# Sixteen-wide heads: query projections without padding, and projections in narrower pieces

## What is computed

```python
def cross(x, ctx, Wq, bq, Wk, bk, Wv, bv, Wo, bo):      # layers 0 and 2
    xn = layernorm(x)                                    # (2, 1024, 256)
    Q, K, V = xn @ Wq + bq, ctx @ Wk + bk, ctx @ Wv + bv # heads of 16
    attn = softmax(Q_h @ K_h.T / 4)                      # 16 heads, 1024 x 77
    return concat(attn @ V_h) @ Wo + bo

def msa(x, w_qkv, w_proj):                               # layer 3
    q, k, v = split(x @ w_qkv)                           # heads of 16
    attn = softmax(q_h @ k_h.T * 0.25)                   # 16 heads, 1024 x 1024
    return concat(attn @ v_h) @ w_proj

x = x + tanh(g) * cross(layernorm(x), ctx, ...)          # layers 0 and 2
x = x + msa(layernorm(x), w_qkv, w_proj)                 # part of layer 3
```

## Time and profile before

| | |
|---|---|
| median of three runs | 3246.15 us (3243.53 to 3255.63) |
| the profiled execution's own time | 3252.0 us |
| its span | 3250.3 us |
| TensorE (PE) busy | 2932.5 us, 90% of the span |
| VectorE (DVE), ScalarE (ACT), GpSimd (POOL) busy | 1639.8, 1269.4, 1286.2 us |
| l0x, about | 5 to 157 us |
| l2x, about | 1500 to 1640 us |
| l3a, about | 2490 to 3015 us |

### The profile page before, as it was taken

How to read it: one execution, slowest core, us unless ns; L and a number is a source line. 1 busy time by engine, 2 the same in 40 slices (tenths; PEclk the granted TensorE clock), 3 DMA queues, 4 the chain that set the end, 5 groups by cost and what they waited for, 6 DMA issues and landing times. The chain is left out here.

```text
span 3250.3 us, 41502 instructions
## 1 busy us (share of the span) xinstructions
PE 2932.5 (90%) x15957; PEld 1574.7 (48%) x15957; DVE 1639.8 (50%) x3314; ACT 1269.4 (39%) x1769; POOL 1286.2 (40%) x1025
## 2 busy tenths in 40 slices
PE   7999899999999999697988999978887888988798
PEld 3565444444434444244466889843333222322587
DVE  4636555554555455485651112246552787786400
ACT  4443444334334443355521111124433465555232
POOL 2232366565666556701243222214656220010433
PEclk9999999999999999898998999989998899999999
DMA  1400000000000000000025455520001000000376
GB/s 55 115 27 28 11 6 6 11 6 6 10 6 6 6 6 1 27 1 29 1 83 192 180 204 199 214 79 5 1 14 33 11 14 7 7 14 1 131 239 174
DMA packets 76855, 175.72 MB, mean 54 GB/s; under 512 B 19549, under 2 KB 54290, under 8 KB 63860
## 3 DMA queue, kind: packets, MB, share of 16 engines
q0 software_dynamic: 21744, 118.63, 10.6%
q1 hardware_dynamic: 54916, 54.43, 5.5%
HBM read 141.70 MB, written 27.64 MB: 52 GB/s over the span
## 5 line engine op out<-in xcount | busy, mean ns | idle before, releaser
L1554 POOL TENSOR_TENSOR l1x_added<-l1x_added,l1x_probs 128x1024 f32<-128x1024 f32 x224 | 527.4, 2355 | 264.2 <-ACT l1x_probs L1825 198.5
L1922 DVE TENSOR_REDUCE l1x_tops<-l1x_ring 128x1 f32<-128x512 f32 x512 | 326.4, 685 | 195.3 <-PE l1x_ring L1634 194.8
L1153 DVE TENSOR_REDUCE l3a_halves<-l3a_ring 128x1 f32<-128x512 f32 x512 | 323.3, 683 | 88.1 <-PE l3a_ring L995 84.3
L1825 ACT ACTIVATE l1x_probs<-l1x_slots 128x1024 f32<-128x1024 f32 x256 | 262.0, 1024 | 239.4 <-PE l1x_slots L1678 237.6
L1112 ACT ACTIVATE l3a_probs<-l3a_slots 128x1024 f32<-128x1024 f32 x256 | 248.1, 1021 | 180.3 <-PE l3a_slots L1016 180.3
L1671 PE MATMUL l1x_slots<-l1x_Q,l1x_K 64*128 64x512 f32 x1152 | 311.0, 617 | 6.7 <-ACT l1x_probs L1823 5.5
L1693 PE MATMUL l1x_pv<-l1x_probs,l1x_V 128*64 128x512 f32 x1152 | 282.3, 606 | 0.0
L1016 PE MATMUL l3a_slots<-l3a_lifted,l3a_K 32*128 32x512 f32 x1024 | 151.6, 641 | 34.5 <-ACT l3a_probs L1112 33.6
L947 POOL TENSOR_TENSOR l3a_OT<-l3a_raw,l3a_rsum 128x512 f32<-128x512 f32 x16 | 20.3, 1268 | 403.5 <-DVE l3a_rsum L1184 403.5
L3561 DVE TENSOR_TENSOR l2f_hh<-l2f_sg,l2f_hid 128x256 f32<-128x256 f32 (+1 forms) x184 | 69.8, 380 | 213.0 <-ACT l2f_sg L3408 197.1
L3408 ACT ACTIVATE l2f_sg<-l2f_hid 128x256 f32<-128x256 f32 (+1 forms) x184 | 64.6, 352 | 286.0 <-PE l2f_hid L3324 276.2
(11 more groups left out here) (709 smaller groups left out, 5188.5 us busy)
## 6 DMA issues: line engine op xcount, KB each, us to landing
l1x_w<-in_l_qkv SPq DMA_DIRECT2D x16, 384.0 KB, 3.1
slots_in<-zeros SPq DMA_DIRECT2D x1, 4992.0 KB, 18.2
l2f_yg<-rows_out SPq DMA_DIRECT2D x8, 512.0 KB, 5.5
l2f_xg<-slots_in SPq DMA_DIRECT2D x15, 272.0 KB
slots_in<-zeros SPq DMA_DIRECT2D x1, 2944.0 KB, 17.9
x<-in_x SPq DMA_DIRECT2D x4, 512.0 KB, 8.7
l1f_w<-in_l_w SPq DMA_DIRECT2D x2, 1024.0 KB, 7.2
x<-x SPq DMA_DIRECT2D x4, 512.0 KB, 2.9
```

Of the source, the lines that this page charges most:

```text
L1153: nc.vector.tensor_reduce(halves[:, k % 2, col:col + 1], bank_of(banks[e]), AX.X, ALU.max).then_inc(s["bank_done"], 1)
L1554: ins = nc.gpsimd.tensor_tensor(added[h][:], added[h][:], probs[:, n % PROBS, :, :], ALU.add)
L1825: ins = nc.scalar.activation(p, s2[m % 2], ACT.Exp)
L1922: ins = nc.vector.tensor_reduce(tops[:, e * NT + t, h:h + 1], bank, AX.X, ALU.max)
```

## The change

Three parts.

1. Both cross attentions: from unit 4 on, the query projection uses dense weights `wq_dense` (new input `qd`), so one projection of 512 columns yields two units. Its result goes to `dense`, and SP spreads it with four DMAs per unit into Q, whose pads are those of the first four units. The projections for units 4, 6, 8, 10, 12 and 14 stand in the units 1 (ahead of the first maxima), 2, 4, 6, 8 and 10. The shifted queries go to buffers of their own (`lifted`). The cast ("low") of u+3 now stands behind the events "part" of u-1.
2. The self attention: the four projections of a pair become 16 of 128 columns, spread over ten steps of three units; the value tiles, outputs and casts get other places.
3. The clearing of the DRAM tables moves from l0x to l0f, behind its weight loads.

```diff
     def query(u, pool=rings):
         job("q", u, pool=pool)
-        events.append(("low", u))
...
         events.append(("score", u))
         if u + 1 < units:
             turn(u + 1)
+        if u == 1:
+            query(4)
         if u + 2 < units:
             maxima(u + 2, 0)
...
         events += side.get(u, [])
-        if u + 3 < units:
-            query(u + 3)
+        if u == 0:
+            query(3)
+        elif u % 2 == 0 and u + 4 < units:
+            query(u + 4)
         if u:
             events += [("part", 0, u - 1), ("part", 1, u - 1)]
+        if u + 3 < units:
+            events.append(("low", u + 3))
         if u >= 5:
             out(u - 5)
...
+            sp.dma_start(wq_dense[:], w["qd"]).then_inc(s["dense_loaded"], 16)
...
+            for u in range(QS, U):
+                sp.wait_ge(s["job_done"], done_by("q", u // 2 * 2))
+                sp.wait_ge(s["shifted"], u - QS + 1)
+                sp.wait_ge(s["low_ready"], u - QS + 1)
+                for j in range(4):
+                    row = 64 * (u % 2) + 16 * j
+                    sp.dma_start(Q[u % QS][32 * j:32 * j + 16, :], dense[u // 2 % 2][row:row + 16, :]).then_inc(spread[u % QS], 16)
...
             def low_query(u):
-                pool.wait_ge(s["job_done"], done_by("q", u))
+                query_done(pool, u)
                 pool.tensor_copy(Qb[u % QS][:], Q[u % QS][:]).then_inc(s["low_ready"], 1)
...
                 for k in range(KD):
-                    last = nc.tensor.matmul(out, wq[:, k, q * P:(q + 1) * P], xT[:, k, n * CH:(n + 1) * CH], start=k == 0, stop=k == KD - 1)
+                    heads = wq[:, k, q * P:(q + 1) * P] if u < QS else wq_dense[:, k, q // 2 * P:(q // 2 + 1) * P]
+                    last = nc.tensor.matmul(out, heads, xT[:, k, n * CH:(n + 1) * CH], start=k == 0, stop=k == KD - 1)
...
     for pair in range(1, units // 4):
-        u = 4 * pair - 4
-        jobs[u, 4], jobs[u, 5] = [("k", pair, 0, CH)], [("k", pair, CH, CH)]
-        jobs[u, 6], jobs[u + 1, 1] = [("q", pair, 0, CH)], [("q", pair, CH, CH)]
...
+        spots = [(4 * pair - 4, i) for i in (3, 5, 6, 7)] + [(4 * pair - 4 + j, i) for j in (1, 2) for i in (1, 2, 3, 5, 6, 7)]
+        parts = [(kind, pair, i * P, P) for kind in "kq" for i in range(NT)]
+        for at, part in zip(spots, parts):
+            jobs[at] = [part]
```

More of the change, by code:

```diff
@@ L240, in plan_cross @@
         query(u, pool=slots)
+        events.append(("low", u))
         if u < 2:
@@ L330, in cross16, with query_done @@
         x_loaded = [c.semaphore(f"{name}_x_loaded{n}") for n in range(NC)]
+        spread = [c.semaphore(f"{name}_spread{i}") for i in range(QS)]
         rows_total = 3 if mask is not None else 1
         block = ctx.enter_context(nc.Block())
+        def query_done(eng, u):
+            if u < QS:
+                eng.wait_ge(s["job_done"], done_by("q", u))
+            else:
+                eng.wait_ge(spread[u % QS], 64 * (u // QS))
         def bank_free(eng, freed):
@@ L479, in scores @@
                     rows = slice(32 * j, 32 * j + 32)
-                    last = nc.tensor.matmul(slots[0:SC, j, :], K[rows, q, b * SC:b * SC + SC], Q[u % QS][rows, :], start=True, stop=True, tile_position=(32 * j, 0))
+                    last = nc.tensor.matmul(slots[0:SC, j, :], K[rows, q, b * SC:b * SC + SC], lifted[u % 2][rows, :], start=True, stop=True, tile_position=(32 * j, 0))
                 last.then_inc(s["score_psum"], 1)
@@ L564, in evacuate @@
                     q = u % QUADS
-                    ins = nc.scalar.activation(Q[u % QS][:], ps, ACT.Identity, bias=bqk[:, q:q + 1], scale=0.25)
+                    if u >= QS + 4:
+                        query_done(act, u - 4)
+                        query_done(act, u - 3)
+                    to, col = (Q[u], q) if u < QS else (dense[u // 2 % 2], 8 + q // 2)
+                    ins = nc.scalar.activation(to[:], ps, ACT.Identity, bias=bqk[:, col:col + 1], scale=0.25)
                 ins.then_inc(s["job_done"], 1)
@@ L608, in norm @@
                     dve.wait_ge(s["bias_loaded"], 16)
+                    step.add(nc.vector.tensor_scalar(bqk[:, 8:10], bqk[:, 8:10], 0.25, None, ALU.mult))
+                    step.wait()
                     nc.vector.tensor_scalar(bqk[:, 0:4], bqk[:, 0:4], 0.25, None, ALU.mult).then_inc(s["bias_ready"], 1)
@@ L2078, in plan0, with ffn0 @@
     return plan
[L2081 removed]
+def ffn0(nc, c, name, gate, io, to_clear=()):
     DH = io["l0_w1h"].shape[1]
@@ L2139, in _ @@
                 sp.dma_start(dst[:], row_tile(src, P)).then_inc(s["b2_loaded"], 16)
+            for rows, spare in to_clear:
+                sp.wait_ge(s["w2_loaded"], 32)
+                sp.wait_ge(s["b2_loaded"], 32)
+                sp.dma_start(rows[:, 0:D].rearrange("(n p) d -> p n d", p=P),
+                             c.zeros[:].unsqueeze(1).broadcast_to([P, rows.shape[0] // P, D])).then_inc(c.cleared, 16)
+                sp.dma_start(rows[:, D:], spare).then_inc(c.cleared, 16)
         @block.gpsimd
@@ L3626, in pack16 @@
     packed = {"q": by_partition(wq if dense else padded(wq)), "k": by_partition(wk if dense else padded(wk)), "v": by_partition(wv), "o": by_partition(out.reshape(2 * D, D)),
-              "bqk": np.concatenate([b.reshape(4, P).T for b in bias], 1)}
+              "bqk": np.concatenate([b.reshape(4, P).T for b in bias] + [(zero if bq is None else bq).reshape(2, P).T], 1)}
+    if not dense:
+        packed["qd"] = by_partition(wq)
     if bv is not None:
@@ L3688, in program @@
         io["scratch"] = nc.dram_tensor("scratch", (TT, P), F32, kind="Internal").ap()
-        cross16(nc, c, "l0x", io["x"], weights(io, "l0x"), 0, io["ctx_t"], mask=io["mask0"], to_clear=[(io[f"slots_in{top}"], io[f"spare_rows{top}"]) for top in (2, 1)])
+        cross16(nc, c, "l0x", io["x"], weights(io, "l0x"), 0, io["ctx_t"], mask=io["mask0"])
         c.end_stage()
-        ffn0(nc, c, "l0f", 4, io)
+        ffn0(nc, c, "l0f", 4, io, to_clear=[(io[f"slots_in{top}"], io[f"spare_rows{top}"]) for top in (2, 1)])
         c.end_stage()
```

41 lines of the change are left out of this document (22 added, 19 removed).

## The result

The changed kernel takes **3268.51 us** in the median (3265.86 to 3270.27, five runs), the kernel before, beside it, 3251.71 (3243.53 to 3255.63, five runs): ratio 1.0053, 95% interval 1.0039 to 1.0067. So it is 0.53% slower, 16.8 us, just over what I had called measurable, and above the range of the prediction. It is also at the figure of two of its rivals, in part by luck: they had +21 and +22 us on a kernel before of 3246.15, which stands at 3251.71 in this comparison. The profiled execution took 3270.27 us, its span is 3268.5.

The account below looks back on a forecast made before the run. PE was taken to bound the kernel, busy 90% of the span. Cross attentions +7.6 us, self attention -7.4 and clearing 0 gave +0.2 on the 3246.15 median, forecast as 3247 us, range 3217 to 3262.

Parts of the forecast that it names:

- two of its rivals: Whole kernel: self attention pieces hide nothing (chance 0.07), or the clock falls at each cross attention pause (0.06); both 3268 us.
- The wait, its chain and the loop: Cross attentions: PE waits for POOL's cast behind DVE's division; early units 6.42 us each, +2.4 us per stage.
- The first rival: Cross attentions: PE does not wait for the cast, both stages save 10.3 us each, total 3219; chance 0.2.
- the sum of my terms for that part: Cross attentions from unit 7 on: -1.8 + 0.2 - 0.74 - 1.72 - 0.72 + 1.0 us.
- The clock: Cross attentions: one and a half falls of the clock behind pauses at 1.4 us, 2.1 per stage; l2x has one already.
- the chain's 2.4 us: Each cross attention: unit 7 starts 6.2 us late, later units win part back, +2.4 us per stage.
- The rival that let the clock fall at each pause: Cross attentions: nine pauses per stage at 1.4 us each, 12.6 instead of 2.1, total 3268; chance 0.06.
- one mild case of two: Cross attentions: of two 2 us pauses in the trace, the projection after that at 58.66 took 1.98 us, nothing slowed.
- The self attention: Self attention: 48 pieces at 0.20 us, 9.6, replace twelve projections worth 17.0, so -7.4 us.
- five dear places of 16: Self attention: five of 16 places per pair stand behind a step with three maxima, a piece there costing up to 0.4 us.
- The second rival: Self attention: pieces hide nothing, 0.66 us per step, the stage loses 14.7, total 3268; chance 0.07.
- The clearing: DRAM tables cleared in l0f instead of l0x: 0 us both ways.

Follow-up runs that it names:

- e1: The change's cross attentions and clearing with the self attention's plan of the kernel before; 3268.67 us, ratio 1.0053 to the kernel before.
- e4: The changed kernel with idle matmuls, five ahead of the wait in unit 2 and three in unit 6 of both cross attentions; 3261.3 us in one execution.
- e2: The kernel before with only the change's self attention plan; 3247.35 us, ratio 0.9981 to the kernel before.
- e6: The changed kernel with the self attention's 128-column pieces in steps 3 to 7 and the value tiles moved off them; 3248.18 us, ratio 1.0028.
- e10: The kernel before with only the clearing of the DRAM tables moved from l0x to l0f; 3237.93 us in one execution.
- e5: The changed kernel with POOL's cast at the head of its unit, ahead of the statistics' factors and the multiplication; 3219.78 us, ratio 0.9939.
- e8: The change with dense queries from the seventh unit on, cast first, and the last chunk's statistics in unit 2 instead of 5; 3207.19 us, ratio 0.9902.
- the first four experiments: Four kernels on one chip: e1, e2, the changed kernel with the cast ahead of the multiplication again, and e4; 3268.67, 3247.35, 3244.55 and 3261.3 us.

## Why the prediction was wrong

**The wait, its chain and the loop: right.** The cast behind the multiplication waits for the division; the maxima of unit 2 at 19.1 us from the first scores in e1 and 19.9 in the change, for 19.2; waits of 14.7 us, the longest 5.2 (I had said 20 and 5); pairs of 5.4 and 8.1, then 6.4. From unit 7 to unit 14 the stage gains 3.8 us on the kernel before (53.5 to 49.7), the sum of my terms for that part to the tenth. The first rival (no wait) is out.

**The clock: the first step that failed**, worth 8.6 of the 14.1 us by which the three stages lie over the forecast. "I take one such fall for the long pause and half of one for the other, 1.5 x 1.4 = 2.1 per stage". All that l0x lost beyond the chain's 2.4 us is 7.8 - 2.4 = 5.4, for which I had 2.1, and it lies before unit 7: 0.7 of it ahead of the maxima of unit 2, 4.7 from there to the scores of unit 7 (37.6 us, forecast 32.8). With the two long pauses filled (e4) that stretch takes 34.3, so their falls make 3.3 of the 4.7. Both brought a fall, in both stages, and each cost more than the 1.4 of the earlier trace rows: there only a projection ran slow, here the values, the second maxima and all of the projection, 2.0 to 3.0 us by e4, of which the loop gave back a part. Shorter pauses brought more, in unit 4 of l0x (behind 2.00 us) and in unit 13 of l2x (behind 1.31). The rival that let the clock fall at each pause came out at the measured time, but not by its count: in l0x three falls behind pauses of the loop, where it had nine, at more than 1.4 each. The fourth, in unit 0, stands behind a pause of 1.40 us that the kernel before has too.

The Trainium skill ("TensorE: Matmul & The Clock Gate", section "What's actually happening") has it that the throttled state is the default and that activity releases it. By that rule a pause may cost more than its length. The traces agree for each of the 16 pauses of 2.8 us or more that the two stages have, from their first scores on, in all the kernels here; under that it went both ways. I had let one mild case of two halve the price.

**The self attention: right in sign, mis-sized**, the other 5.5 of the 14.1 us. "I take 0.20: 48 x 0.20 = 9.6, so -7.4 us". The pieces of a pair cost 0.73 + 2.02 + 2.02 = 4.77 us over bare steps, 0.30 each, 14.3 for all. Against the 17.0 that I had for the projections that is -2.7 (counted in the same way, by steps, the twelve projections cost 17.6: -3.3), and the stage gained 1.9 (2.4 in e2). The 0.20 was the cost of a piece in a step with nothing else; I had counted five dear places of 16, at up to 0.4, with which the mean would have been up to 0.25, and still took 0.20; measured, four of six cost 0.36 to 0.70. The rest did not go to the value tiles, which cost 5.7 us in all for 5.5 before; 0.3 went to the outputs and about 1 to the first three units of the stage, where steps wait in both kernels. The second rival (0.66 each) is out too. Why a piece costs near a quarter of a projection on average, in either order, is not settled: e6 excludes the division as the only cause.

**The clearing: right**, 0 by e10. **The spreading transfers: right for the change**, where the cast came later than they did; wrong as a general statement, since with the cast first they are what unit 2 waits for (e5).

**The sum.** +7.8 and +8.4 and -1.9 are +14.3, against the forecast's +0.2; the medians differ by 16.8. What is left, 2.5 us, is within what the untouched stages differ by between traces. So the expected gain of 10.3 us of projections per cross attention was first turned into a wait on POOL, and then more than spent by the clock behind that wait. With queries dense only once there is time for them, the cast first and the statistics early, both stages gain 9.8 and 11.1 us (e8), with five projections fewer, not six: in l0x the five units without them are 1.71 or 1.72 us shorter each, and shorter waits give the rest.

## What to carry to other kernels

When work is taken off the engine that bounds a stage, list which in-order engine now has to be early, and put the small operation that the bounding engine waits for ahead of the large one that nobody waits for. Price a pause of TensorE at its length and the slow stretch behind it, 2 to 3 us here after a pause of 3 to 5, and fill or remove it first. Start a cheaper path with a longer latency only where the pipeline already has slack.

## What the runs showed of the hardware

- The granted clock fell behind a pause of 1.3 us (unit 10 of e4, unit 13 of l2x in the change) and stayed at full behind one of 2.1 (unit 2 of l0x in the kernel before). In one execution the same unit took 8.60 us at a granted clock of 1.00 and 13.10 at 0.74; the same instructions of l2x fell behind a pause of 2.03 us in the kernel before (0.83 over the unit) and kept their clock behind 2.02 in e10.
- Matmuls whose results nobody reads were worth their place in a pause here: ten recorded ones (4.46 us) ahead of the maxima brought those behind them from 1.94 and 3.18 us to 1.07 and 1.98, and the stages were 2.5 and 4.4 us shorter, in one execution.
- Stages without any edit differ from chip to chip by as much as this change is worth: l2f takes 492.4 to 493.1 us in the traces of the two kernels and of the first four experiments, and 474.4 to 481.1 in those of the six on the two other chips. So only ratios to the kernel before on the same chip can be read at this size, and even these with the stages beside them: e6, whose three edited stages together lie 14.8 us above the kernel before (14.3 in the change), has a ratio of 1.0028 where the change has 1.0053.
